# Reordering the steps of a fused conditioning, token-picking and feed-forward kernel

## The reference

```
ctx      = ema(x, tau_ctx)                        # h[t] = a*h[t-1] + x[t]
gated    = x * sigmoid([x, ctx] @ Wg.T + bg)
mod      = 0.5 + sigmoid(gelu(x @ Wn1.T + bn1) @ Wn2.T + bn2)     # 128 dendrites
traces_d = ema(gated * mod_d, tau_d)              # for each dendrite d
temporal = sum_d softmax(blend)_d * traces_d
out      = (gelu(x @ Wsoma.T + bsoma) * sigmoid(temporal @ Wtemp.T + btemp)) @ Wout.T
o        = layernorm(out) * gamma + beta
pick the 16 of 32 tokens with the highest o . w_router;  h = gelu(o_picked @ W1 + b1) @ W2 + b2
result   = x + o + scatter(sigmoid(score) * h)
```

## Time and profile before

| | us |
|---|---|
| median of 3 runs | 177.65 (177.19 to 177.79) |
| the profiled execution | 177.13 |
| its span, first to last instruction | 175.3 |
| PE busy | 164.5 |
| DVE busy | 132.8 |
| POOL busy | 128.7 |
| ACT busy | 93.1 |

### The profile page before, as it was taken

How to read it: one execution, slowest core, us unless ns; L and a number is a source line. 1 busy time by engine, 2 the same in 40 slices (tenths; PEclk the granted TensorE clock), 3 DMA queues, 4 the chain that set the end, 5 groups by cost and what they waited for, 6 DMA issues and landing times.

```text
span 175.3 us, 3161 instructions
## 1 busy us (share of the span) xinstructions
PE 164.5 (94%) x1076; PEld 125.1 (71%) x1076; DVE 132.8 (76%) x188; ACT 93.1 (53%) x160; POOL 128.7 (73%) x129
## 2 busy tenths in 40 slices
PE   6779999999999999999889999999999999899991
PEld 6654558596557685798564779787939869888881
DVE  2378798978985987987999798788866666868413
ACT  3185996675614724553353943525275479567420
POOL 7906904998335899689999998999889849199900
PEclk9999999999999999999999999999999999999999
DMA  3995000000000000000000000000000040040214
GB/s 78 265 266 146 0 4 0 0 0 2 6 0 0 0 4 0 0 4 0 0 0 0 4 0 2 0 4 0 0 6 0 0 122 4 0 120 0 85 38 120
DMA packets 12767, 5.60 MB, mean 32 GB/s; under 512 B 2864, under 2 KB 12624, under 8 KB 12752
## 3 DMA queue, kind: packets, MB, share of 16 engines
q1 hardware_dynamic: 11840, 5.20, 11.5%
q10 hardware_dynamic: 912, 0.20, 0.7%
HBM read 3.30 MB, written 2.10 MB: 31 GB/s over the span
## 4 chain that ended last, share of the span: by engine, by line
PE 72%; DVE 11%; issue 4%; POOL 4%; DMA 3%; ACT 2%; SPq 0%; DVEq 0%; POOLq 0%
PE ring L1085 21%; PE ring L1158 6%; PE ring L1140 5%; POOL ctx_acc L507 4%; PE ring L1057 4%; PE ring L1101 4%; PE ring L1068 3%; PE ring L1041 3%; PE ring L1042 3%; PE ring L1020 3%; DMA x_nat<-in_x_dram 3%; PE ring L1168 3%; PE ring L1109 3%; DVE mod_lo L814 2%; PE ring L1095 2%
## 5 line engine op out<-in xcount | busy, mean ns | idle before, releaser
L507 POOL TENSOR_TENSOR ctx_acc<-ctx_acc,prod 128x640 f32<-128x640 f32 (+10 forms) x44 | 69.1, 1580 | 15.2 <-DVE prod L847 11.5
L847 DVE TENSOR_TENSOR prod<-ring,gm 128x640 f32<-128x640 f32 (+10 forms) x44 | 34.8, 818 | 7.3 <-PE ring L1085 6.1
L1085 PE MATMUL ring<-mod_hi,decayed_lo 128*128 128x512 f32 (+7 forms) x80 | 25.0, 377 | 1.1 <-DVE state L834 0.8
L1085 PE MATMUL ring<-mod_hi,decayed_hi 128*128 128x512 f32 (+7 forms) x80 | 22.5, 346 | 0.0
L1085 PE MATMUL ring<-mod_lo,decayed_hi 128*128 128x512 f32 (+7 forms) x80 | 22.5, 346 | 0.0
L834 DVE TENSOR_TENSOR state<-ring,blend_w 128x1024 f32<-128x1024 f32 x16 | 18.8, 1217 | 1.8 <-PE ring L1057 1.8
L1085 PEld LDWEIGHTS ring<-mod_hi,decayed_lo 128*128 128x128 f32 x80 | 13.9, 188 | 7.5 <-issue 5.4
L1085 PEld LDWEIGHTS ring<-mod_lo,decayed_hi 128*128 128x128 f32 x80 | 14.5, 188 | 1.2 <-issue 0.2
L1158 PE MATMUL ring<-w_sb,gm 128*128 128x128 f32 x128 | 15.2, 276 | 0.0
L1085 PEld LDWEIGHTS ring<-mod_hi,decayed_hi 128*128 128x128 f32 x80 | 14.5, 188 | 1.0
L1158 PEld LDWEIGHTS ring<-w_sb,gm 128*128 128x128 f32 x128 | 14.8, 192 | 0.3 <-ACT gm L710 0.2
(11 more groups left out here) (168 smaller groups left out, 360.3 us busy)
## 6 DMA issues: line engine op xcount, KB each, us to landing
x_nat<-in_x_dram SPq DMA_DIRECT2D x4, 512.0 KB, 5.0
out_dram<-x_nat SPq DMA_DIRECT2D x3, 512.0 KB, 3.2
...
bn<-in_L_cond_bn_dram ACTq DMA_DIRECT2D x4, 0.1 KB, 4.2
```

What stands on the lines that cost most here:

```text
L507: nc.gpsimd.tensor_tensor(dst, dst, packed(prod[:, n % NP, 0:width(r)], r, k), ALU.add).then_inc(acc_done, 1)
L847: nc.vector.tensor_tensor(dst, packed(slot(step), r, k), lagged(gated(r), r, k), ALU.mult).then_inc(read(step), 1)
L1085: last = nc.tensor.matmul(to[:, c], w[:, k, :], src[:, c], start=(i == 0), stop=(i == len(parts) - 1))
```

## The change

The string `ORDER` is replaced by another; the 230 steps in it are the same, and nothing else changes. On every engine the same instructions are issued in another order, and the ring of banks is dealt out in the new order. The places that the prediction speaks of, old and new:

```diff
 ORDER = """
-decay:0 powers:0 decays:0 xt:0 turn_b:0 context:0 turn_a:0 xt:1 plus_beta:0 h1:0 soft:0 turn_c:0 context:1
-turn_f:0 wg:0 mod:0 gated:0 h1:1 table:0.0 table:0.1 table:0.2 low:0 split:0 ffn_w:0 table:0.3 mod:1 wg:1
-gated:1 early:0 unit:0.0 unit:0.6 unit:0.4 unit:0.7 split:1 xt:2 soma:0 h1:2 context:2 unit:0.8 low:1 unit:0.1
...
-unit:1.3 plus_beta:1 back:0.0 state:1.0 unit:1.1 gate:0 soma_gate:0 nat:2.1 turn_e:0 carry:1.0 h1:3 carry:1.1
-low:2 mod:3 unit:1.10 unit:1.6 unit:1.4 back:1.0 unit:1.5 out:0.0 unit:1.7 nat:2.0 stats:0.0 unit:2.0
-plus_beta:2 sum:1 unit:2.1 split:3 unit:2.11 unit:2.9 out:0.1 low:3 back:1.1 stats:0.1 state:2.1 soma:1 unit:3.0
...
-residual:0 unit:3.11 unit:3.6 back:2.0 carry:3.0 carry:3.1 score:1 bc:1 tie:1 soma_gate:2 pick:1 normed:1 gate:2
-sum:3 back:3.1 down:0 back:3.0 out:2.0 gather:1 scatter:0 stats:2.0 out:2.1 stats:2.1 gate:3 up:1.0 up:1.1 var:2
...
+decay:0 decays:0 xt:0 turn_b:0 powers:0 context:0 soft:0 turn_a:0 xt:1 turn_c:0 context:1 h1:0 rw:0 wg:0 gated:0
+ffn_w:0 table:0.0 mod:0 table:0.1 split:0 table:0.2 h1:1 low:0 turn_d:0 table:0.3 wg:1 gated:1 mod:1 unit:0.0
+low:1 unit:0.3 split:1 unit:0.4 xt:2 early:0 context:2 unit:0.1 soma:0 unit:1.0 unit:0.11 unit:0.6 unit:0.9
+nat:0.1 nat:0.0 unit:0.2 turn_f:0 turn_e:0 state:0.1 xt:3 wg:2 context:3 plus_beta:0 duo:1.12 unit:0.8 gated:2
+unit:0.10 early:1 plus_beta:1 unit:1.9 unit:1.4 state:0.0 wg:3 duo:1.13 unit:1.5 duo:1.15 h1:2 carry:0.0 mod:2
...
+sum:0 split:2 back:0.0 mod:3 early:2 low:2 state:1.0 unit:1.2 unit:2.0 unit:1.3 unit:2.2 state:1.1 unit:1.1
+gate:0 unit:2.8 split:3 soma_gate:0 unit:1.10 nat:2.1 sum:1 carry:1.1 carry:1.0 state:2.1 low:3 var:0 soma:1
+out:0.0 stats:0.0 unit:2.10 out:0.1 nat:2.0 back:1.0 stats:0.1 unit:2.4 back:1.1 state:2.0 carry:2.1 unit:3.0
...
+duo:3.13 turn_pick:0 state:3.0 unit:3.2 duo:3.15 carry:3.1 carry:3.0 duo:3.14 normed:1 back:3.1 score:1 back:3.0
+unit:3.4 sum:2 up:0.1 residual:0 bc:1 unit:3.1 tie:1 unit:3.7 up:0.0 soma_gate:2 sum:3 pick:1 gate:2 down:0
+out:2.1 gather:1 var:2 stats:2.1 scatter:0 residual:1 out:2.0 gate:3 stats:2.0 turn_pick:1 plus_beta:2
...
 """
```

More of the change, by code:

```diff
@@ L60 @@
 ORDER = """
-decay:0 powers:0 decays:0 xt:0 turn_b:0 context:0 turn_a:0 xt:1 plus_beta:0 h1:0 soft:0 turn_c:0 context:1
-turn_f:0 wg:0 mod:0 gated:0 h1:1 table:0.0 table:0.1 table:0.2 low:0 split:0 ffn_w:0 table:0.3 mod:1 wg:1
-gated:1 early:0 unit:0.0 unit:0.6 unit:0.4 unit:0.7 split:1 xt:2 soma:0 h1:2 context:2 unit:0.8 low:1 unit:0.1
-mod:2 unit:0.2 nat:0.1 unit:0.5 nat:0.0 unit:1.0 early:1 unit:0.9 duo:1.14 xt:3 context:3 state:0.1 wg:2
-duo:1.13 duo:1.12 nat:1.1 carry:0.1 gated:2 state:0.0 duo:1.15 rw:0 unit:0.11 wg:3 unit:0.10 gated:3 nat:1.0
@@ L66 @@
-unit:1.8 unit:0.3 unit:1.9 back:0.1 unit:1.2 turn_d:0 early:2 split:2 state:1.1 carry:0.0 sum:0 unit:1.11
-unit:1.3 plus_beta:1 back:0.0 state:1.0 unit:1.1 gate:0 soma_gate:0 nat:2.1 turn_e:0 carry:1.0 h1:3 carry:1.1
-low:2 mod:3 unit:1.10 unit:1.6 unit:1.4 back:1.0 unit:1.5 out:0.0 unit:1.7 nat:2.0 stats:0.0 unit:2.0
-plus_beta:2 sum:1 unit:2.1 split:3 unit:2.11 unit:2.9 out:0.1 low:3 back:1.1 stats:0.1 state:2.1 soma:1 unit:3.0
-unit:2.6 var:0 unit:3.4 unit:2.5 early:3 nat:3.1 state:2.0 gate:1 carry:2.1 soma_gate:1 score:0 carry:2.0
@@ L71 @@
-unit:3.9 unit:2.8 unit:3.10 normed:0 unit:3.3 unit:2.10 bc:0 tie:0 out:1.1 stats:1.1 soma:2 nat:3.0 duo:3.12
-unit:2.7 unit:2.2 unit:3.8 duo:3.15 pick:0 back:2.1 out:1.0 duo:3.13 soma:3 unit:3.5 stats:1.0 unit:2.3 unit:2.4
-unit:3.7 gather:0 state:3.1 up:0.1 var:1 unit:3.1 duo:3.14 turn_pick:0 state:3.0 up:0.0 sum:2 unit:3.2
-residual:0 unit:3.11 unit:3.6 back:2.0 carry:3.0 carry:3.1 score:1 bc:1 tie:1 soma_gate:2 pick:1 normed:1 gate:2
-sum:3 back:3.1 down:0 back:3.0 out:2.0 gather:1 scatter:0 stats:2.0 out:2.1 stats:2.1 gate:3 up:1.0 up:1.1 var:2
@@ L76 @@
-residual:1 soma_gate:3 normed:2 turn_pick:1 score:2 out:3.0 bc:2 tie:2 pick:2 var:3 stats:3.0 residual:2 down:1
-out:3.1 stats:3.1 gather:2 scatter:1 up:2.0 up:2.1 score:3 normed:3 plus_beta:3 bc:3 tie:3 pick:3 turn_pick:2
-down:2 gather:3 scatter:2 up:3.0 up:3.1 turn_pick:3 down:3.0 down:3.1 scatter:3.0 residual:3 scatter:3.1
+decay:0 decays:0 xt:0 turn_b:0 powers:0 context:0 soft:0 turn_a:0 xt:1 turn_c:0 context:1 h1:0 rw:0 wg:0 gated:0
+ffn_w:0 table:0.0 mod:0 table:0.1 split:0 table:0.2 h1:1 low:0 turn_d:0 table:0.3 wg:1 gated:1 mod:1 unit:0.0
@@ new lines @@
+low:1 unit:0.3 split:1 unit:0.4 xt:2 early:0 context:2 unit:0.1 soma:0 unit:1.0 unit:0.11 unit:0.6 unit:0.9
+nat:0.1 nat:0.0 unit:0.2 turn_f:0 turn_e:0 state:0.1 xt:3 wg:2 context:3 plus_beta:0 duo:1.12 unit:0.8 gated:2
+unit:0.10 early:1 plus_beta:1 unit:1.9 unit:1.4 state:0.0 wg:3 duo:1.13 unit:1.5 duo:1.15 h1:2 carry:0.0 mod:2
+gated:3 h1:3 carry:0.1 duo:1.14 unit:0.7 back:0.1 unit:1.11 unit:0.5 nat:1.0 nat:1.1 unit:1.8 unit:1.6 unit:1.7
+sum:0 split:2 back:0.0 mod:3 early:2 low:2 state:1.0 unit:1.2 unit:2.0 unit:1.3 unit:2.2 state:1.1 unit:1.1
@@ new lines @@
+gate:0 unit:2.8 split:3 soma_gate:0 unit:1.10 nat:2.1 sum:1 carry:1.1 carry:1.0 state:2.1 low:3 var:0 soma:1
+out:0.0 stats:0.0 unit:2.10 out:0.1 nat:2.0 back:1.0 stats:0.1 unit:2.4 back:1.1 state:2.0 carry:2.1 unit:3.0
+unit:3.9 unit:2.5 unit:3.3 gate:1 score:0 early:3 soma_gate:1 back:2.1 carry:2.0 unit:2.3 unit:2.9 normed:0
+unit:3.6 bc:0 unit:2.1 out:1.1 soma:3 tie:0 back:2.0 pick:0 unit:3.5 unit:2.7 stats:1.1 nat:3.1 unit:3.11
+unit:2.6 out:1.0 unit:3.8 nat:3.0 duo:3.12 stats:1.0 var:1 gather:0 state:3.1 unit:2.11 unit:3.10 soma:2
@@ new lines @@
+duo:3.13 turn_pick:0 state:3.0 unit:3.2 duo:3.15 carry:3.1 carry:3.0 duo:3.14 normed:1 back:3.1 score:1 back:3.0
+unit:3.4 sum:2 up:0.1 residual:0 bc:1 unit:3.1 tie:1 unit:3.7 up:0.0 soma_gate:2 sum:3 pick:1 gate:2 down:0
+out:2.1 gather:1 var:2 stats:2.1 scatter:0 residual:1 out:2.0 gate:3 stats:2.0 turn_pick:1 plus_beta:2
+soma_gate:3 up:1.0 up:1.1 normed:2 out:3.0 var:3 score:2 bc:2 tie:2 pick:2 stats:3.0 residual:2 down:1 out:3.1
+stats:3.1 gather:2 scatter:1 up:2.0 score:3 up:2.1 plus_beta:3 bc:3 normed:3 turn_pick:2 tie:3 pick:3 down:2
@@ L79 @@
+gather:3 scatter:2 up:3.0 up:3.1 turn_pick:3 down:3.0 down:3.1 scatter:3.0 scatter:3.1 residual:3
 """
```

## The result

The changed kernel takes 175.85 us (median of 6 runs, 175.65 to 176.68) against 177.60 before (6 runs): a ratio of 0.9915, 95% interval 0.9892 to 0.9939, so 1.75 us faster. In a second measurement, beside more runs of the kernel before, it is 176.06 against 177.65, ratio 0.9922 (0.9896 to 0.9947). The forecast was 176.4. The profiled execution took 176.68, the longest of its six, with a span of 174.9. Four executions further down (three of the kernel before, one of a variant) fell into a slower state, and medians and ratios leave them out.

What follows compares the result with a forecast made beforehand. The prediction took PE, busy 164.5 of 175.3 us, as the bound, with POOL second. Head +0.8 and middle -2.0 made -1.2 on 177.13, so 175.9, or 176.4 as median; own range 175.3 to 177.0, overall 174.7 to 178.8.

Steps and rivals of the forecast that it cites:

- The sum: Whole kernel: +0.8 - 2.0 = -1.2 us on the profiled 177.13 gives 175.9; the median 0.5 above that, 176.4.
- The middle: PE between 82.51 and 89.22: 2.0 us of waiting go as POOL and DVE are no longer late; bounds 0 to 2.5.
- The signs: If right: `unit:0.0` near 25.0, three `mod_lo` at 1.2 us, PE idle under 0.5 between 75 and 95, `sum:2`/`gate:2` near 129.5.
- One reading of the middle: PE's gaps of 0.80 and 0.84 us at 83.92 and 89.22: DVE in `low:3` for 2.72 us just ahead of both.
- The head: Start up to the first lag: ACT's longer chain makes `unit:0.0` about 0.8 us later; bounds 0.3 to 1.4.
- POOL's account: POOL's additions up to `sum:2`: +1.9 - 4.7 - 1.0 + 4 = +0.2 us, ending at 129.4, just in time for `gate:2`.
- The wait of `sum:1`: POOL's queue ahead of `unit:2.10`: `sum:1` waits for `back:1.1`, 0 to 6 us, taken as 4.
- rival 1: POOL becomes the bound, `sum:1` waiting 6 us: 178.3, some 180 without `plus_beta` cover; decides above 4 us; chance 0.20.
- signs of a wrong forecast: POOL idle over 5 us ahead of `sum:1`, PE waiting at `gate:2` or `gate:3`, or matmuls at twice their length behind `ffn_w`.
- Rival 4: PE's middle: more goes than the two gaps, since POOL is ahead until `sum:1`; 175.0, chance 0.10.
- Rival 2: `low:2` still meets POOL's additions, the collision only moves; a 2.1 us wait eats the gain: 177.3 to 177.9, chance 0.20.
- Rival 3: TensorE's clock falls in the head between `wg:0` and `wg:1`: `wg:1` costs 3.8 us more, 180.2; chance 0.05.

## Why the prediction was right, and where not

**The sum.** The forecast was 176.4, 1.2 us below the kernel before; the two measurements have 175.85 and 176.06, 1.75 and 1.6 below. That the number is so near is in part luck: by the traces both terms were too large, with opposite signs, and PE's clock and the first lag move single executions by as much as the terms' errors. The trace before (177.13) is one of the fastest of its kernel and the trace after (176.68) the longest of its six, so terms read from single traces don't add up to the medians to better than about 0.5 us.

**The middle, -2.0 us: right in place, near in size, half right in its cause.** From the first lag to `gate:3` the three traces with the order after, or with only `sum:1` moved in it, are 1.6 to 1.7 us shorter than the kernel before. The prediction named four things that should free the stretch from 68 to 90: `low:1` and `low:3` moved, and two `plus_beta` gone. The runs need only the `plus_beta`: they give -2.0 and -2.1 us in two measurements with the subtractions where they stood. The subtractions moved in the old order cost some 3 us, and the order after with the `plus_beta` put back is 1.1 to 1.4 us above the kernel before. What the rest of the new string gains or costs was not tried step by step. The signs came: three of four subtractions were to be at 1.2, and all are at 1.2 to 1.3; PE has no idle time above 0.5 us between 75 and 95, and the windows from 70 to 100 lack 0.09 us in all.

**One reading of the middle was wrong.** The prediction has DVE in `low:3` just ahead of both gaps and ACT's copy ending the first. The first gap runs from 83.12 to 83.92, and `low:3` begins inside it, at 83.58. With `low:3` at 1.22 us (`:2` moved) the gap stands unchanged. It belongs to the late product ahead of `low:3`, and through it to `low:2` at 70.82, twelve microseconds earlier. For the second gap the reading was right.

**The head, +0.8 us: the chain is right, the size not settled.** Without a fall of the clock the first lag begins at 24.54, so +0.36 against 24.18, near the lower bound of 0.3, and what PE waits for there is DVE's small read of `turn_d`, as forecast. But the old head alone spreads from 24.18 to 24.92 over six traces, and the new one from 24.54 to 25.28 over the five that have it unchanged, with and without a fall of the clock; the means differ by 0.6. In the profile of the section on the result the first lag comes at 25.28, close to the forecast's 25.0, but for another reason: the head ran ahead until PE's clock fell in `wg:1`, whose first two pairs took 2.05 and 1.69 us, not 1.02 each. The prediction measured the new head against an old one that holds the tables' collision. Taking `plus_beta:0` out of it without the new order of the head gives 174.89; the order after takes all three out of the same places and needs some 1.1 us more (0.9922 against 0.9857). The first lags differ by as much (24.54 - 23.44); that the new head is the cause is argued from these two rows, and wasn't tried by itself.

**POOL's account: the end right by luck, two terms wrong.** First addition 30.2 forecast, 30.37 measured; `sum:2` to end at 129.4, ended at 129.10. The wait of `sum:1` was 6.70, not 4, beyond the point from which rival 1 was to decide. It didn't decide: the sum let the whole wait go through to `sum:2`, and it didn't. With the additions of round 2 some 2.7 us earlier nothing changes, so POOL was not "just in time" but had slack; that `sum:2` ended where it was forecast is not due to the account. Two of the three signs of a wrong forecast were seen, idle time above 5 us ahead of `sum:1` and matmuls at twice their length behind `ffn_w`, and the forecast held all the same.

**The rivals.** Rival 1 gives some 180 when the cover of the two `plus_beta` is gone; by its own terms (178.3 + 4.7) it is 183. Rival 4 (more goes than the two gaps of 0.80 and 0.84 us) did not come in the order after; with the two `plus_beta` alone 2.1 us go.

Rival 2 (the collision only moves): a loss of 2.1 us on the forecast is 178.5, not 177.3 to 177.9. In the order after the collision does move, to POOL's side, 0.8 us at 66.43, and PE does not feel it. The Trainium skill (SBUF — State Buffer, section "SBUF: two separate sides") lets the engine that starts first keep the shared port for its whole instruction, when DVE's has two inputs in SBUF and POOL's reads SBUF. The rows agree: `low:3` behind `plus_beta` ends 1.09 us after it in two kernels (84.21 and 83.33 above), and the addition that starts 0.16 us after `low:2` takes 3.01 us for 896 columns (2.12 in the order after). But who loses the port is not yet who loses time.

Rival 3 (the clock falls in the head) was given 0.05 and a price of 3.8 us. The mean clock is below 1.00 in seven of twelve executions, and in some of the kernel before too, at 0.2 to 1.7 us: in the two traces of the changed kernel the level comes back within `wg:0` or `wg:1`. The chance was far too low and the price too high, and the two errors partly offset each other. The prediction's reading of the eight transposes at 9.45 (1.73 us) as the lower level is not borne out: the windows view of that trace has a granted clock of 1.00 from 9.4 to 11 us. Why they were slower there stays open; in the trace after the same eight took 1.09 us at 9.21.
